# Graph layer and expert FFN on one core: experts' 16-bit halves joined by VectorE, input halves ahead of low parts, sums ahead of new weights, requests by GpSimd

## The reference

```python
h = layernorm(x) @ gnn_W.T + gnn_b          # graph layer: sums over edges, scaled by degrees
x = x + segment_sum(norm * h[col], row)
t = layernorm(x) @ lin0_w + lin0_b
t = silu(t @ swi1_w1 + swi1_b1) * (t @ swi1_w2 + swi1_b2)
routed = sum over the 4 best of 8 experts: w_e * (silu(t @ exp_w1) * (t @ exp_w3)) @ exp_w2
shared = (silu(t @ sh_w1) * (t @ sh_w3)) @ sh_w2       # hidden width 2048
t = (routed + shared) @ lin1_w + lin1_b
t = silu(t @ swi2_w1 + swi2_b1) * (t @ swi2_w2 + swi2_b2)
x = x + t
```

## Time and profile before

| | us |
|---|---|
| median of 3 runs | 1546.89 (1545.82 to 1547.36) |
| the profiled execution's own time | 1547.93 |
| its span, first to last instruction | 1546.3 |
| PE busy | 1517.0 (98%), 10412 products |
| PE weight loads (PEld) busy | 1498.4 (97%) |
| DVE busy | 838.5 (54%) |
| ACT busy | 649.8 (42%) |
| POOL busy | 115.0 (7%) |
| granted TensorE clock, mean | 0.996 of full |

### The profile page before, as it was taken

How to read it: one execution, slowest core, us unless ns; L and a number is a source line. 1 busy time by engine, 2 the same in 40 slices (tenths; PEclk the granted TensorE clock), 3 DMA queues, 4 the chain that set the end, 5 groups by cost and what they waited for, 6 DMA issues and landing times.

```text
span 1546.3 us, 27037 instructions
## 1 busy us (share of the span) xinstructions
PE 1517.0 (98%) x10412; PEld 1498.4 (97%) x10412; DVE 838.5 (54%) x1396; ACT 649.8 (42%) x934; POOL 115.0 (7%) x139
## 2 busy tenths in 40 slices
PE   9999999999999999999999999999999799999998
PEld 8998999999999999999999999999999799999998
DVE  8664569854533345454545455555553256345886
ACT  6322335542222344454444445454444475223442
POOL 1321010000100000001010100000000330001000
PEclk9999999999999999999999999999999899999999
DMA  4412212233522568888797878888768664221333
GB/s 138 135 42 68 68 42 86 94 111 120 143 83 82 147 182 214 218 190 238 191 241 197 239 205 226 213 208 251 190 189 203 183 183 121 91 69 56 102 113 84
DMA packets 168029, 230.04 MB, mean 149 GB/s; under 512 B 110580, under 2 KB 119330, under 8 KB 167914
## 3 DMA queue, kind: packets, MB, share of 16 engines
q1 hardware_dynamic: 142044, 182.07, 43.8%
q0 software_dynamic: 14976, 33.08, 7.2%
q10 hardware_dynamic: 10894, 13.26, 2.7%
HBM read 185.28 MB, written 18.95 MB: 132 GB/s over the span
## 4 chain that ended last, share of the span: by engine, by line
PE 84%; DVE 6%; ACT 4%; issue 3%; DMA 2%; ACTq 1%; POOL 0%; DVEq 0%; POOLq 0%
PE acc L1886 79%; PE acc L1866 3%; ACT w_hi L553 1%; DMA act_x<-y_dram,top_idx 1%; DVE yrow L1708 1%; ACT work L1013 1%; ACT gath L1056 1%; DVE w_lo L1357 1%; DVE work L1652 1%; ACT yrow L1056 1%; PE acc L1935 0%; DVE w_lo L1306 0%; DVE yrow L1122 0%; DMA y_dram<-yrow 0%; DVE yrow L1121 0%
## 5 line engine op out<-in xcount | busy, mean ns | idle before, releaser
L1886 PE MATMUL acc<-act_x,w_hi 128*128 128x312 f32 (+8 forms) x2304 | 509.1, 310 | 4.6 <-ACT act_x L985 3.9
L1886 PE MATMUL acc<-act_b,w_hi 128*128 128x312 f32 (+8 forms) x2048 | 449.7, 309 | 0.0
L1886 PE MATMUL acc<-act_a,w_hi 128*128 128x314 f32 (+1 forms) x1920 | 424.8, 311 | 14.8 <-ACT work L848 12.1
L1306 DVE TENSOR_TENSOR w_lo<-raw,w_hi 128x1024 fp32r<-128x1024 f32 x253 | 309.1, 1222 | 209.8 <-ACT w_hi L553 203.7
L1886 PEld LDWEIGHTS acc<-act_x,w_hi 128*128 128x128 f32 x2304 | 386.4, 189 | 7.2 <-issue 6.2
L1886 PE MATMUL acc<-act_x,w_lo 128*128 128x312 f32 (+8 forms) x1152 | 356.4, 309 | 0.0
L1886 PEld LDWEIGHTS acc<-act_b,w_hi 128*128 128x128 f32 x2048 | 342.2, 189 | 0.1
L1886 PEld LDWEIGHTS acc<-act_a,w_hi 128*128 128x128 f32 x1920 | 321.2, 191 | 17.2 <-ACT work L848 13.1
L1886 PE MATMUL acc<-act_b,w_lo 128*128 128x314 f32 (+8 forms) x1024 | 315.5, 308 | 0.0
L1886 PE MATMUL acc<-act_a,w_lo 128*128 128x314 f32 (+1 forms) x960 | 295.8, 308 | 0.0
L553 ACT ACTIVATE w_hi<-raw 128x1024 fp32r<-128x1024 f32 x264 | 276.9, 1050 | 5.6 <-PE acc L1886 4.6
(11 more groups left out here) (230 smaller groups left out, 1119.2 us busy)
## 6 DMA issues: line engine op xcount, KB each, us to landing
raw<-stream_dram SPq DMA_DIRECT2D x296, 512.0 KB, 3.9
y_dram<-yrow POOLq DMA_DIRECT2D x16, 512.0 KB, 6.0
y_dram<-yrow POOLq DMA_DIRECT2D x8, 352.0 KB, 7.3
rows<-x_dram ACTq DMA_DIRECT2D x1, 2500.0 KB
x_dram<-rows ACTq DMA_DIRECT2D x5, 500.0 KB
h_rows_dram<-rows ACTq DMA_DIRECT2D x1, 2500.0 KB
rows<-x_dram ACTq DMA_DIRECT2D x8, 312.5 KB
rows<-x_dram SPq DMA_DIRECT2D x5, 448.0 KB
```

Of the source, the lines that this page charges most:

```text
L1306: dve.tensor_tensor(w_lo[:, s, :], raw[:, s, :], w_hi[:, s, :].bitcast(f32), ALU.subtract).then_inc(lo_split, count)
L1886: ins = pe.matmul(o, w, xs_[h], start=(first and w is hi and xs_ is x_hi), stop=(last and w is lo))
```

## The change

1. **Outputs joined by VectorE, per expert.** New `y_rows(e)`: VectorE joins the halves of the transposed outputs into `grow` (in `gath`), three copies of up to 128 x 2048 16-bit elements, at m = 1 of the next expert; the last expert's follow its down units. `y_dram` now holds floats, `save_y` stores `grow` tile by tile as `y_words` counts. ScalarE's `back_rows` is gone: the gathers of the second shared half write to the slots that VectorE reads, and ask for a slot again when VectorE has used it. `add_back`, `add_tile` and the turns stand one pair later.
2. **Inputs.** `x_stage` has three tiles, so the three gathers of the next expert go out together. The transposes stand after loads 14, 16 and 18; the first waits for all three gathers and for the store of the outputs before, since both use `gath`. In the down units `expert_in_word` stands ahead of `weight_low`.
3. **Seven-product layers, block q = 1.** VectorE's second and third sum come ahead of the sums and low parts for block 2, which are spread over the rest of the block; ScalarE saves `p1` ahead of its first high part for block 2.
4. **Requests.** `fetch_x1` and the four pairs of `store` move from ScalarE's program to the end of GpSimd's, with a semaphore of their own (`pairs_saved`).

The diff, cut to its core:

```diff
-X_TURNS = (11, 15, 19)
+X_TURNS = (14, 16, 18)
-    y_dram = nc.dram_tensor("y_dram", (EXPERTS * CAP, 2 * D), u16).ap()
+    y_dram = nc.dram_tensor("y_dram", (EXPERTS * CAP, D), f32).ap()
-        x_stage = flat_b[:, 9 * D:10 * D].bitcast(u16)
+        x_stage = flat_b[:, 2 * KC * CAP:2 * KC * CAP + 3 * D].bitcast(u16).rearrange("p (n d) -> p n d", n=3)
...
             def turn_inputs(e, n, source, count):
+                if e >= 2 and n == 0:
+                    sp.wait_ge(y_saved, 16 * 3 * (e - 1))
             def turn_outputs(e, m):
-                    sp.wait_ge(y_saved, 16 * 3 * e)
+                    sp.wait_ge(y_words, 3 * e)
...
-                        turn_inputs(r + 1, n, x_stage, 3 * (r + 1) + n + 1)
+                        turn_inputs(r + 1, n, x_stage[:, n, :], 3 * (r + 2))
...
             def save_y(e):
-                for s in range(2):
-                    pool.wait_ge(y_turned[s], e * (8 * KC) + 8 * KC)
-                pool.sem_inc(save_go, 1)
                 for n, (c0, cn) in enumerate(SLOT_TILES):
+                    pool.wait_ge(y_words, e * 3 + (n + 1))
+                    pool.sem_inc(pool_go, 1)
                     pool.dma_start(y_dram[bass.ds(e * CAP + c0, cn), :],
-                                   y_halves[0:cn, :, n, :]).then_inc(y_saved, 16)
+                                   grow[0:cn, n, :]).then_inc(y_saved, 16)
...
             with pool.Fori(1, EXPERTS - 1) as e:
                 pool.wait_ge(x32_ready, e * KC + KC)
                 gather_list(e + 1)
-                gather_tile(x_stage, 0)
+                for n in range(3):
+                    gather_tile(x_stage[:, n, :], n)
                 save_y(e - 1)
-                gather_rest(e + 1)
...
                     if i >= 1:
-                        pool.wait_ge(back_words, TOP * (i - 1) + k + 1)
-                    pool.indirect_dma_start(out=back_parts[0:TT, k, :, :].rearrange("p t d -> p (t d)"), out_offset=None,
-                                            in_=y_dram,
+                        pool.wait_ge(back_used, TOP * (i - 1) + k + 1)
+                    pool.indirect_dma_start(out=back_slot(k), out_offset=None, in_=y_dram,
...
+            pool.wait_ge(t_sum, len(TWO) * HK)
+            for p in range(HK):
+                fetch_x1(p)
+            pool.wait_ge(o_rows, 4)
+            store(0, NT, 0, 2 * P)
+            store(0, NT, HK * P, (HK + 2) * P)
+            pool.wait_ge(o_rows, 6)
+            store(0, NT, 2 * P, 3 * P)
+            store(0, NT, (HK + 2) * P, (HK + 3) * P)
...
             for m in range(KC):
                 gated_pair(shb, m, b_hi, None)
-                if m < NT:
-                    back_rows(m)
...
             for m in range(KC):
+                expert_in_word(0, m)
                 weight_low(U_SHA, UNITS_UP + m + 3)
-                expert_in(0, m)
-            expert_in_lo(0, KC - 1)
+                expert_in_lo(0, m)
+
+            def y_rows(e):
+                for s in range(2):
+                    dve.wait_ge(y_turned[s], e * (8 * KC) + 8 * KC)
+                for n, (c0, cn) in enumerate(SLOT_TILES):
+                    dve.tensor_copy(grow[0:cn, n, :].bitcast(u16).rearrange("p (d t) -> p t d", t=2),
+                                    y_halves[0:cn, :, n, :]).then_inc(y_words, 1)
...
                     weight_low(base, 2 * m + 3)
+                    if prev and m == 1:
+                        dve.wait_ge(x32_ready, e * KC + KC)
+                        y_rows(e - 1)
...
                 gated_pair(shb, m, b_hi, b_lo, None)
-                if 2 <= m < NT + 2:
-                    add_tile(m - 2)
-                if 1 <= m <= NT:
-                    add_back(m - 1)
+                if 3 <= m < NT + 3:
+                    add_tile(m - 3)
+                if 2 <= m < NT + 2:
+                    add_back(m - 2)
```

More of the change, by code:

```diff
@@ L327, in build @@
         out_saved = sem("out_saved")
+        pairs_saved = sem("pairs_saved")
         class Stage:
@@ L708, in _, with fetch_x1, store @@
             quad_lows(TWO[1])
+            def fetch_x1(p):
+                if p >= 1:
+                    pool.wait_ge(x1_back, 32 * p)
+                for m in (p, p + HK):
+                    pool.dma_start(rows[0:TT, :, m * P:(m + 1) * P], x1_tiles[:, :, m * P:(m + 1) * P]
+                                   ).then_inc(x1_back, 16)
+            def store(i0, i1, c0, c1):
+                for r0, r1 in ((0, SPREAD), (SPREAD, TT)):
+                    pool.dma_start(out_tiles[r0:r1, i0:i1, c0:c1], rows[r0:r1, i0:i1, c0:c1]).then_inc(pairs_saved, 16)
+            pool.wait_ge(t_sum, len(TWO) * HK)
[7 more added lines that the diff above has]
+            store(0, NT, (HK + 2) * P, (HK + 3) * P)
         @block.scalar
@@ L905, in quads @@
                     more = q + 1 < KC
-                    if more:
+                    if more and q != 1:
                         quad_high(L, q + 1, 0)
@@ L1049, in _ @@
                 act.wait_ge(ov_added, 2 * NT)
[L1051 to L1055, removed]
-                    act.activation(back_slot(k).bitcast(u16).rearrange("p (d t) -> p t d", t=2),
-                                   back_parts[0:TT, k, :, :], ACT.Copy).then_inc(back_words, 1)
             for m in range(KC):
                 gated_pair(shb, m, b_hi, None)
-                if m < NT:
-                    back_rows(m)
             for m in range(KC):
@@ L1068, in _ @@
             linear_high(TWO[1])
-            def fetch_x1(p):
-                if p >= 1:
-                    act.wait_ge(x1_back, 32 * p)
-                for m in (p, p + HK):
-                    act.dma_start(rows[0:TT, :, m * P:(m + 1) * P], x1_tiles[:, :, m * P:(m + 1) * P]
-                                  ).then_inc(x1_back, 16)
-            fetch_x1(0)
-            def store(i0, i1, c0, c1):
-                for r0, r1 in ((0, SPREAD), (SPREAD, TT)):
-                    act.dma_start(out_tiles[r0:r1, i0:i1, c0:c1], rows[r0:r1, i0:i1, c0:c1]).then_inc(out_saved, 16)
-            def fetch_next(q):
-                if q % 2 == 1 and q + 1 < KC:
-                    fetch_x1(q // 2 + 1)
-                if q == 5:
-                    act.wait_ge(o_rows, 4)
-                    store(0, NT, 0, 2 * P)
-                    store(0, NT, HK * P, (HK + 2) * P)
-            quads(TWO[1], lambda q: None, lambda q: None, fetch_next)
-            act.wait_ge(o_rows, 6)
-            store(0, NT, 2 * P, 3 * P)
-            store(0, NT, (HK + 2) * P, (HK + 3) * P)
+            quads(TWO[1], lambda q: None, lambda q: None, lambda q: None)
             for count, i0, i1, m in LAST_STORES:
@@ L1417, in product, with second_sum @@
                                                  in1=silu4[:, c], op0=ALU.add, op1=ALU.mult).then_inc(L.gated.prod, 1)
-                    if more and q >= 1:
+                    def second_sum():
+                        dve.wait_ge(p1_saved, L.p1 + q + 1)
+                        dve.wait_ge(quad_done, L.quads + quads_until(q, 1))
+                        dve.tensor_tensor(u2, acc[:, 1, 0:HT], p1, ALU.add).then_inc(u_done, 1)
+                    if more and q >= 2:
                         sums_first(L, q + 1)
                         quad_low(L, q + 1, 0)
-                    dve.wait_ge(p1_saved, L.p1 + q + 1)
-                    dve.wait_ge(quad_done, L.quads + quads_until(q, 1))
-                    dve.tensor_tensor(u2, acc[:, 1, 0:HT], p1, ALU.add).then_inc(u_done, 1)
+                    second_sum()
                     def third_sum():
@@ L1432, in quad_sums @@
                         sums_first(L, 1, third_sum)
+                    elif q == 1:
+                        third_sum()
+                        sums_first(L, 2)
+                        quad_low(L, 2, 0)
                     else:
@@ L1441, in quad_sums @@
                         quad_low(L, 1, 0)
-                    elif more:
+                    elif more and q >= 2:
                         quad_low(L, q + 1, 2)
@@ L1696, in _ @@
             expert(EXPERTS - 1, False)
+            dve.wait_ge(y_saved, 16 * 3 * (EXPERTS - 1))
+            y_rows(EXPERTS - 1)
             def add_back(i):
                 for k in range(TOP):
-                    dve.wait_ge(back_words, TOP * i + k + 1)
+                    dve.wait_ge(back[k], 16 * (i + 1))
                     w = top_w[0:TT, k, i:i + 1]
```

54 lines of the change are left out of this document (24 added, 30 removed).

## The result

| | before | changed |
|---|---|---|
| median | 1546.36 us (4 runs, 1545.30 to 1547.36) | 1519.72 us (4 runs, 1519.25 to 1520.32) |
| ratio | | 0.9828 (95% interval 0.9811 to 0.9845) |
| profiled execution, its span | 1547.93, 1546.3 us | 1519.96, 1518.3 us |
| granted clock, mean | 0.996 | 1.000 |

The account below looks back on a forecast made before the run. TensorE, busy 98% of the span, was taken as the bound, so only its waits and slow clock could be won. Terms sum to 26.2 us off 1547.93, giving 1521.7, or 1520.7 us as median; range 1517 to 1530.

Parts of the forecast that it names:

- Second shared half: Taking 20 copies off ScalarE ends 13.1 us of TensorE's silu waits and 2.5 us of slow clock: -15.6 us.
- Copies on VectorE: In the experts, output copies of 1.4 us each, 4.2 a block, fit VectorE's waiting time, covered by 8 us: 0.
- Experts' starts: New order in the down units removes 6.2 us of waits and 1.2 us of slow stretch: -7.4 us.
- the ring: Down units: ScalarE and VectorE wait for each other, 3.84 us a round; the new order makes it 2.2.
- Transfers: Next inputs' gathers go out together, transposes after loads 14, 16, 18; some 8 us cover SP holding a load: 0.
- the slower rival: Outputs' store holds SP's queue, so the transpose and weight loads wait; six experts lose 5 us each: 1551 us, chance 0.03.
- Seven-product layers: Second block: earlier sums end TensorE's 2.8 us of waits in two layers, 0.4 us a layer given back: -2.0 us.
- Requests: Moving requests from ScalarE to GpSimd ends the wait at the turn of rows at 1523.8 us: -1.2 us.
- The gathers bound the second shared half: Rival, chance 0.10: formula 0.3 + landing + 1.3 us must fit in 14.8 us; landing in 15 us gives 1525.7.
- GpSimd's requests hold VectorE up: Rival, chance 0.05: sixteen requests in a layer where VectorE has no gap cost it time: 1521 to 1535 us.
- The order does not do what it says: Rival, chance 0.06: experts' starts still wait, for the copy or for late transposes: 1528 us.
- the copies are slow: Rival, chance 0.04: VectorE's output copies take 3 us each, 9 us against a cover of 8, seven times: 1530 to 1540.

Follow-up runs that it names:

- number 11: The changed kernel run once more, unedited, beside numbers 9 and 10: 1521.55 us median.
- number 5: Kernel before, with only the 20 copies of the second shared half moved from ScalarE to VectorE, in the same place: 1540.28 us.
- number 3: Changed kernel with the three copies of each expert's outputs done twice: 1521.49 us.
- Numbers 1: Changed kernel with the old order put back in the down units, low part of the weights ahead of the copy of inputs: 1527.12 us.
- number 2: Kernel before with only the new order of copy, low part and low half in the down units: 1538.29 us.
- number 6: Changed kernel with the transposes of the next inputs after loads 7, 9 and 11 instead of 14, 16 and 18: 1536.31 us.
- Number 9: Changed kernel with block 2 of both seven-product layers treated as block 1, third sum and output step earlier: 1519.33 us.
- Number 8: Changed kernel with the x1 fetches and the four pairs of stores requested by ScalarE again: 1522.77 us.
- Number 10: Changed kernel with a token tile's gathers requested only when all four slots of the tile before are used: 1537.18 us.

## Why the prediction was right, point by point

**The sum.** 26.2 us were forecast and 26.2 us are measured from product 626 on. The mechanisms were right, but that the figures agree to the tenth is luck. The errors of the terms cancel: the experts' starts gave 0.65 us more, the seven-product layers 0.5 less. And the sum was drawn up from one execution of the kernel before and is compared with that same one, while its runs lie between 1543.0 and 1549.4 us; by medians the gain is 26.6 us in the result and 24.7 us beside number 11.

**Second shared half (-15.6; measured 15.8).** The reason holds: ScalarE was the bound there by its queue. What the prediction put at nothing, the copies in their new place, is what makes the term: number 5 leaves them in that half and gets 4.7 us (5.8 by medians). Four rounds of the changed kernel, as in the earlier trace rows:

```profile
1238.75:1253.50 14.75, 14.75 (x106) 14.74 (x105) 9.43 (x11) 3.32 (x4) 5.75 (x4) 1.00 0.88 189
1253.50:1268.40 14.90, 14.90 (x108) 14.89 (x106) 9.58 (x11) 3.33 (x4) 6.47 (x4) 1.00 0.85 215
1268.40:1283.20 14.80, 14.80 (x108) 14.79 (x105) 9.48 (x11) 3.32 (x4) 6.00 (x4) 1.00 0.77 213
1283.20:1298.00 14.80, 14.80 (x108) 14.79 (x105) 9.47 (x11) 3.32 (x4) 0.48 (x1) 1.00 0.48 145
```

A round takes 14.8 us where one took 16.5, and PE has no gap. VectorE's work is 9.5 us, as reckoned from the earlier trace rows.

**Copies on VectorE (0; measured 0).** The estimate of 1.4 us from the earlier trace rows was good:

```profile
L1662 DVE COPY gath<-yrow x24: 1317/1342/1359, 608.4 to 1190.1; 128x2048 uint16<-128x2048 uint16 x16, 88x2048 uint16<-88x2048 uint16 x8
```

It is the line through both rows (1.3), not the proportion (1.66), that held. One detail was missed. VectorE, in the expert of the earlier trace rows as it now is:

```profile
949.88 1.23 DVE L1286 TENSOR_TENSOR w_lo<-raw,w_hi 128x1024 fp32r<-128x1024 f32 x1
952.83 3.79 DVE L1662 COPY gath<-yrow 128x2048 uint16<-128x2048 uint16 x3 [1.72 <-DMA yrow<-work]
956.50 0.50 DVE L1676 TENSOR_TENSOR work<-acc,work 128x344 f32<-128x344 f32 x1
```

The copies wait 1.72 us for the last transpose of the outputs, which landed late (median 4.2 us, up to 11.2). So the product behind is 1.7 us late (two units of 3.47 us after 947.86 would be 954.8), not under 1 us. The cover took it, and 3.8 us more (number 3).

**Experts' starts (-7.4; measured 8.05).** Numbers 1 and 2 show the ring and nothing else. The output copies stand 3.3 to 3.8 us apart now, at TensorE's pace. The gain at the starts grows as the experts shrink: 0.4, 0.6, 1.2, 1.6 and 4.1 us at the last five. Of the 0.65 us that the sum had too little, 0.4 belong to the last start: products come late from 1115.2 us on (two waits, 2.5 us, and 1.6 us of slow pace), and the prediction counted the slow pace from 1116.30 on, 1.2 us. The others are small gaps, 0.1 of them ahead of the experts.

**Transfers (0; measured 0).** SP's queue isn't held by the store: see number 6, which also shows the slower rival's mechanism at work once the transposes come seven loads earlier.

**Seven-product layers (-2.0; measured 1.5).** The waits went, but 0.4 us a layer was given back in my sum, and the traces show 0.34 and 0.75: in the second layer the turn of rows in block 2 then waits for VectorE's rows (L1822). The term missed that VectorE in this layer has the output rows on top, ahead of which a turn stands. Number 9 moves two operations behind them and has it back.

**Requests (-1.2; measured 1.1).** Number 8 gives the same 1.1 us from the other side.

**The rivals.** *The gathers bound the second shared half* was the nearest miss. The gathers, and VectorE's waits in that half:

```profile
DMA to landing us min/median/max: 8.4/11.7/16.7
```

```profile
DVE yrow L1708 <- DMA yrow<-y_dram,top_idx: 9.4, 3, 5.1
DVE yrow L1708 <- DMA gath<-y_dram,top_idx: 4.9, 3, 2.2
```

In the earlier trace rows it was 9.9 and at most 13.1 us; the worst is now above the limit of the prediction's formula (13.2 us), and VectorE waits 14.3 us in all. TensorE did not wait, since these waits fell on VectorE's idle time; afterwards VectorE waited only 2.30, 1.87, none and 2.20 us for TensorE in the four rounds. Landing over 13 us was one of the prediction's own signs of being wrong; it came, and cost nothing. Number 10 shows what lies behind that edge. A chance of 0.10 was not too much. *GpSimd's requests hold VectorE up* is refuted for the layer that it names by number 8 and by the rows of the last section. *The order does not do what it says* and *the copies are slow* are refuted by numbers 1 and 2, and by the 1.34 us of a copy.

## What to carry to other kernels

When a queue of one engine is the bound, ask not only which other engine is free, but in which stage: the same copies of 1.34 us cost nothing in the experts and took about two thirds of the gain away in the shared half. Two engines that hand a unit to each other and back in every round have a period of their own; write down its steps, and put what needs no hand-over ahead of what does. To compare two traces of a full TensorE, subtract the starts of the same product: it separates the change's terms from what one execution does differently at its start.

## What the runs showed of the hardware

**GpSimd's requests wait for VectorE, which hardly waits for them.** POOL and DVE of the changed kernel in the second shared half:

```profile
1227.89 2.17 POOL L694 DMA_INDIRECT gath<-y_dram,top_idx  x1 [23.12 <-DVE yrow L1705]
1230.36 1.19 POOL L694 DMA_INDIRECT gath<-y_dram,top_idx  x1 [0.30 <-issue]
1231.86 2.11 POOL L694 DMA_INDIRECT gath<-y_dram,top_idx  x1 [0.30 <-DVE yrow L1708]
```

```profile
1227.70 2.67 DVE L1708 SCALAR_TENSOR_TENSOR yrow<-gath,top_w,yrow 125x1024 f32<-125x1024 f32 x2
1230.48 1.28 DVE L1708 SCALAR_TENSOR_TENSOR yrow<-yrow,top_w 125x1024 f32<-125x1024 f32 x1
1231.68 1.22 DVE L1286 TENSOR_TENSOR w_lo<-raw,w_hi 128x1024 fp32r<-128x1024 f32 x1
```

A gather's request that starts 0.2 to 0.4 us into such an operation of VectorE takes 1.9 to 2.2 us, one that starts before it, in its last 0.2 us or beside none takes 1.19 to 1.29; VectorE's own times don't move in these rounds. Under the row of copies of number 5 a request took 4.41 us:

```profile
1275.09 4.41 POOL L703 DMA_INDIRECT act_x<-y_dram,top_idx  x1 [8.16 <-DVE gath L1701]
```

So the prediction read the earlier trace rows too broadly: there the request had started first. The Trainium skill (SBUF — State Buffer, "Who interferes with whom") says that issue order decides who blocks, and that the second waits until the first is done; these rows agree for a request that comes second. They show no wait of VectorE where it is the second: its sum at 1230.48 starts within the request of 1230.36 and takes its usual 1.28. The nearest to a wait is in number 5, where an operation with one source, 0.74 us long in the other four rounds, took 0.95 beside a request:

```profile
1229.59 0.95 DVE L1709 TENSOR_SCALAR yrow<-gath,top_w 125x1024 f32<-125x1024 f32 x1
```

VectorE does wait where GpSimd computes. At the start of the first seven-product layer, before and after the change, GpSimd makes low parts, and two sums of VectorE take 1.23 us each instead of 0.70 (changed kernel):

```profile
207.49 3.98 POOL L611 TENSOR_TENSOR w_lo<-raw,w_hi 128x256 fp32r<-128x256 f32 x4 [72.22 <-ACT w_hi L876]
208.50 1.23 DVE L1318 TENSOR_TENSOR acc<-raw 128x512 f32<-128x512 f32 x1
```

Plain requests for transfers are not shown to cost VectorE anything: beside two of 1.65 us each at 1428.33 VectorE's sums of weights took 0.70, 0.69 and 0.69 us, to the hundredth what they took before.

**A start in two forms.** With the same code, product 626 starts at 90.1 to 90.8 us in seven of thirteen traces and at 92.4 us or later in the others. The difference is made in the first sums over edges. A stretch of PE, before and changed:

```profile
7.40:11.00 3.60, 3.60 (x17) 3.21 (x17) 1.20 (x4) 2.94 (x5) 0.00 (x0) 1.00 1.06 264
7.40:11.00 3.60, 3.60 (x29) 3.60 (x28) 2.88 (x9) 2.78 (x6) 0.00 (x0) 1.00 1.06 265
```

17 products start where the other execution starts 29, although the granted clock reads 1.00 in both; in number 2, the latest of all, the slower pace lasts until about 13 us. What decides between the forms was not tried.
